# A decoder layer's convolution: 12 odd heads from stored halves in three rounded passes, the others over two shared buffer sets

## What is computed

```python
# k = v = ctx, q = layernorm(x); B = 8, H = 32 heads of 8 channels, L = 512
kv = einsum('bhil,bhjl->bijhl', k_, v_)          # products of channels i, j of a head
y = irfft(rfft(kv, 2 * L) * rfft(ssm_kernel, 2 * L))[..., :L]   # causal convolution over l
out = y + kv * D
out = einsum('bijhl,bhil->bjhl', out, q_)
```

## Time and profile before

| | us |
|---|---|
| median of three runs | 862.4 |
| the three runs | 861.37, 862.4, 862.54 |
| the profiled execution | 863.55 |
| its span, first to last instruction | 861.8 |

### The profile page before, as it was taken

How to read it: one execution, slowest core, us unless ns; L and a number is a source line. 1 busy time by engine, 2 the same in 40 slices (tenths; PEclk the granted TensorE clock), 3 DMA queues, 4 the chain that set the end, 5 groups by cost and what they waited for, 6 DMA issues and landing times.

```text
span 861.8 us, 14219 instructions
## 1 busy us (share of the span) xinstructions
PE 842.3 (98%) x4346; PEld 704.0 (82%) x4346; DVE 543.4 (63%) x849; ACT 377.3 (44%) x608; POOL 445.9 (52%) x439
## 2 busy tenths in 40 slices
PE   8999999999999999999999999999999999999995
PEld 7888888889877777778888778888888888888884
DVE  6767767775657777888769875544455544555431
ACT  5313322333133533442552255555655555655552
POOL 1233223331068899884622343666666666656644
PEclk9999999999999999999999999999999999999998
DMA  8711101100026543440210397989999888999866
GB/s 283 241 39 21 29 24 37 37 12 13 1 62 196 163 131 110 123 131 17 93 63 7 104 323 171 218 204 215 191 189 214 212 213 195 189 196 223 205 119 86
DMA packets 55109, 114.21 MB, mean 133 GB/s; under 512 B 10721, under 2 KB 14817, under 8 KB 54945
## 3 DMA queue, kind: packets, MB, share of 16 engines
q1 hardware_dynamic: 38048, 73.28, 27.6%
q0 software_dynamic: 17024, 40.48, 25.6%
HBM read 83.07 MB, written 30.67 MB: 132 GB/s over the span
## 4 chain that ended last, share of the span: by engine, by line
PE 90%; DVE 5%; issue 2%; POOL 1%; ACT 1%; POOLq 0%; DVEq 0%; ACTq 0%
PE PS L206 20%; PE PS L208 20%; PE PS L207 20%; PE PS L217 17%; PE PS L1645 4%; PE PS L704 2%; PE PS L695 2%; PE PS L633 1%; PE PS L638 1%; PE PS L1582 1%; PE PS L1572 1%; PE PS L1612 1%; PE PS L1581 1%; PE PS L1564 1%; DVE KV L491 0%
## 5 line engine op out<-in xcount | busy, mean ns | idle before, releaser
L206 PE MATMUL PS<-QY_rounded,wh 128*128 128x512 f32 (+1 forms) x376 | 153.8, 409 | 0.0
L208 PE MATMUL PS<-QY_rounded,wl 128*128 128x512 f32 (+1 forms) x376 | 146.4, 389 | 0.0
L1360 POOL DMA_INDIRECT out_y<-QY,idy x72 | 114.5, 1590 | 44.7 <-ACT QY L1454 33.5
L207 PE MATMUL PS<-QY_rounded,wh 128*128 128x512 f32 (+1 forms) x312 | 120.1, 385 | 0.0
L1916 DVE TENSOR_TENSOR hTl<-hh,hTh 128x512 fp32r<-128x512 f32 (+1 forms) x39 | 27.5, 705 | 107.6 <-ACT hTh L1435 107.6
L1337 POOL DMA_INDIRECT xg<-xs_d,idx x64 | 76.7, 1199 | 28.8 <-POOL idx L1333 13.7
L208 PEld LDWEIGHTS PS<-QY_rounded,wl 128*128 128x128 f32 x376 | 71.1, 189 | 15.1
L217 PE MATMUL PS<-qER,Tz 128*128 128x288 f32 x320 | 81.1, 407 | 0.6 <-DVE QY L1062 0.4
L217 PE MATMUL PS<-prod,Tz 128*128 128x288 f32 x320 | 80.5, 407 | 0.2 <-DVE term L1045 0.2
L206 PEld LDWEIGHTS PS<-QY_rounded,wh 128*128 128x128 f32 x376 | 71.3, 190 | 11.1
L1454 ACT ACTIVATE QY<-PS,WPOS 128x512 f32<-128x512 f32 x76 | 52.4, 690 | 55.1 <-PE PS L208 55.1
(11 more groups left out here) (238 smaller groups left out, 1868.8 us busy)
## 6 DMA issues: line engine op xcount, KB each, us to landing
ws<-in_gu_w SPq DMA_DIRECT2D x38, 512.0 KB, 5.6
ws<-in_dn_w SPq DMA_DIRECT2D x20, 512.0 KB, 6.9
C<-in_ctx SPq DMA_DIRECT2D x32, 256.0 KB, 2.6
Tz<-kpad_d SPq DMA_DIRECT2D x32, 256.0 KB, 3.3
xs_d<-xn SPq DMA_DIRECT2D x16, 256.0 KB, 2.0
out_y<-X SPq DMA_DIRECT2D x16, 256.0 KB, 5.7
X<-in_x SPq DMA_DIRECT2D x1, 3072.0 KB, 16.6
xn<-in_xT SPq DMA_DIRECT2D x6, 512.0 KB, 3.3
```

The costliest lines, as they stand in the source:

```text
L206: pe.matmul(out_, lh, rh, start=first, stop=False)
L207: pe.matmul(out_, lh, rl, start=False, stop=False)
L208: return pe.matmul(out_, ll, rh, start=False, stop=last)
L1360: nc.gpsimd.indirect_dma_start(out=out, out_offset=bass.IndirectOffsetOnAxis(ap=idy[:, t:t + 1], axis=0), in_=yo[:, t], in_offset=None, co ...
```

## The change

1. Heads 7, 9, ..., 29 (`HALVES`, 12 of them) are made in three passes of rounded matmuls (`convolve_halves`), 30 of 288 columns each, from high and low halves of the products and of the padded kernel. They have buffers of their own (`odd_h`, `odd_l`, `TzHi`, `TzLo`, two of each), loaded by `load_halves`: four DMAs a head, two of 256 KB and two of 576 KB.
2. The halves of the products are made in the attention part, two heads in each of the steps 1 to 6, and kept in DRAM (`prod_hl_d`): GpSimd makes the products (three instructions a head), ScalarE copies them rounded into a part of `QY` that is not yet used, GpSimd subtracts that from the products in place, and SyncE stores both and loads the next context. The halves of all padded kernels (`kpad_hl_d`) are made once by GpSimd.
3. The other 20 heads (`WHOLE`) stay plain matmuls. Buffers `Tz`, `C2`, `prod` follow their place in that list and not their parity; PSUM banks still follow the parity.
4. The means read back (`mr`) go to `Tz[0]` instead of the last batch of `QY`. Products 0 to 2 are made after the loop. Several weight semaphores are merged into `w_hi` and `w_lo`. The loops of the convolution are written out. The shared low halves are made in six pieces of 512 columns in place of three of 1024. Warming matmuls read weights in place of `aTl`, with the same shape and count.

The diff, cut to its core:

```diff
+AHEAD = 2
+HALVES = [2 * m + 1 for m in range(3, 3 + AHEAD * (B - DIRECT))]
+WHOLE = [h for h in range(CH) if h not in HALVES]
...
-        mr = QY[:, 0:TPB, B - 1]
+        mr = Tz[0][:].rearrange("p (t n) -> p t n", t=TPB)
...
+        NPROD = B * NPAIR
+        ahead_high = QY[:].rearrange("p c b s -> p c (b s)")[:, :, (B - 2) * S:(B - 2) * S + NPROD]
+        ahead_prod = prod[0][:].rearrange("p c b n -> p c (b n)")
+        AHEAD_MADE, AHEAD_LOW, AHEAD_STEP = (3, 7), (4, 8), 8
...
-        def products(pool, i, k):
-
-            pool.wait_ge(c2_in[k], 16 * (i + 1))
-            pool.wait_ge(conv_ps[k], DC * i)
+        def whole_done(eng, n):
+            h = WHOLE[n]
+            eng.wait_ge(conv_ps[h % 2], DC * (h // 2 + 1))
+
+        def products(pool, n):
+
+            k = n % 2
+            pool.wait_ge(c2_in[k], 16 * (B - DIRECT + n // 2 + 1))
+            if n > 1:
+                whole_done(pool, n - 2)
...
+            def store_half(j, m, half, done):
+                sp.dma_start(prod_hl_d[j, bass.ds(m, 1)].rearrange("o p (c n) -> (o p) c n", c=DC), half).then_inc(done, 16)
...
+            def ahead_batch(b, last=False):
+                n = b * AHEAD - DIRECT * AHEAD
+                made = b * AHEAD_STEP - DIRECT * AHEAD_STEP
+                for j in range(AHEAD):
+                    sp.wait_ge(ahead_hi, n + (j + 1))
+                    store_half(0, n + j, ahead_high, hi_out)
+                    sp.wait_ge(ahead, made + AHEAD_MADE[j])
+                    if last:
+                        load_context(sp, WHOLE[j], j)
+                    else:
+                        ahead_context(n + AHEAD + j, j)
+                    sp.wait_ge(ahead, made + AHEAD_LOW[j])
+                    store_half(1, n + j, ahead_prod, lo_out)
...
+            with sp.Fori(DIRECT, B - 1) as b:
+                turned_batch(b)
+                ahead_batch(b)
...
+            def products_ahead(j, s):
+                pool.wait_ge(c2_in[j], s * 16 + 16)
+                wait_apart(pool, lo_out, s * (16 * AHEAD) + 16 * j)
...
+                for half in range(2):
+                    shifted = bass.AP(tensor=a.tensor, offset=a.offset + 2 * half, ap=[a.ap[0], a.ap[1], [1, 2], [1, CD]])
+                    nc.gpsimd.tensor_tensor(o[:, :, 2 * half * CD:2 * (half + 1) * CD].rearrange("p a (s j) -> p a s j", s=2),
+                                            a[:, :, 0:CD].unsqueeze(2).broadcast_to([P, LB, 2, CD]), shifted,
+                                            ALU.mult).then_inc(ahead, 1)
+                nc.gpsimd.tensor_tensor(o[:, :, 4 * CD:], a[:, :, 0:4], a[:, :, 4:8], ALU.mult).then_inc(ahead, 1)
+
+            def low_ahead(j, s):
+                wait_apart(pool, ahead_hi, s * AHEAD + j + 1)
+                nc.gpsimd.tensor_tensor(ahead_prod.bitcast(F32R), ahead_prod, ahead_high, ALU.subtract).then_inc(ahead, 1)
...
             with pool.Fori(DIRECT - 1, B - 1) as b:
                 rstd(pool, 0, b + 1, mv[0][:, :, 1])
+                s = b - (DIRECT - 1)
+                products_ahead(0, s)
+                low_ahead(0, s)
                 wait_apart(pool, xt_mr_in, 32 * b)
...
+                products_ahead(1, s)
                 rstd(pool, 1, b - 1)
+                low_ahead(1, s)
+            wait_apart(pool, lo_out, 16 * len(HALVES))
+            products(pool, 0)
             pool.wait_ge(qp_done, B)
-            products(pool, 0, 1)
+            products(pool, 1)
...
+            def high_ahead(b, j):
+                n = b - (DIRECT - 1)
+                wait_apart(act, ahead, n * AHEAD_STEP + AHEAD_MADE[j])
+                wait_apart(act, hi_out, n * (16 * AHEAD) + 16 * j)
+                act.activation(ahead_high.bitcast(F32R), ahead_prod, ACT.Copy).then_inc(ahead_hi, 1)
...
                 q_evac(b, first)
...
+                if made_ahead:
+                    high_ahead(b, 0)
                 k_evac(b)
...
                         qy_evac(b - 2)
+                    high_ahead(b, 1)
...
+                def load_halves(n):
+                    k = n % 2
+                    for j, (t, dst) in enumerate(((TzHi[k], odd_h[k]), (TzLo[k], odd_l[k]))):
+                        src = bass.AP(tensor=kpad_hl_d.tensor, offset=(j * CH + HALVES[n]) * (KPAD + 1), ap=[[1, P], [1, D]])
+                        sp.dma_start(t[:], src).then_inc(halves_in[k], 16)
+                        sp.dma_start(dst[:].rearrange("p c b n -> p (c b n)"), prod_hl_d[j, n]).then_inc(halves_in[k], 16)
+
+                def next_heads(i):
+
+                    for h in (2 * i, 2 * i + 1):
+                        sp.wait_ge(conv_ps[h % 2], DC * (i + 1))
+                        if h in HALVES:
+                            n = HALVES.index(h) + 2
+                            if n < len(HALVES):
+                                load_halves(n)
+                        else:
+                            n = WHOLE.index(h) + 2
+                            if n < len(WHOLE):
+                                load_toeplitz(sp, WHOLE[n], n % 2)
+                            if 0 < h and n + 1 < len(WHOLE):
+                                sp.wait_ge(prod_done[(n - 1) % 2], 2 * ((n - 1) // 2 + 1))
+                                load_context(sp, WHOLE[n + 1], (n + 1) % 2)
...
+                next_heads(0)
+                load_halves(0)
                 next_heads(1)
+                load_halves(1)
                 sp.dma_start(gw[:], gateT.rearrange("(c p) n -> p c n", p=P)).then_inc(gw_in, 16)
...
+                def convolve_halves(h, behind=None):
+                    n, m = HALVES.index(h), h // 2
+                    k = n % 2
+                    pe.wait_ge(halves_in[k], 64 * (n // 2 + 1))
+                    pe.wait_ge(y_read[1], 2 * m)
+                    for c in range(DC):
+                        o = PS[:, DC + c].rearrange("p (b n) -> p b n", n=YGAP)[:, :, 0:NPAIR]
+                        for r in range(c + 1):
+                            w = slice((c - r) * P, (c - r + 1) * P)
+                            mm = three_pass(pe, o, TzHi[k][:, w].bitcast(F32R), TzLo[k][:, w].bitcast(F32R), odd_h[k][:, r].bitcast(F32R), odd_l[k][:, r].bitcast(F32R), r == 0, r == c)
```

More of the change, by code:

```diff
@@ L328, in _ @@
             pool.wait_ge(xns[1], TPB * B)
-            products(pool, 1, 0)
+            products(pool, 2)
         @block_.scalar
@@ L380, in qy_evac @@
                                    ACT.Copy).then_inc(qy_done, 1)
+            def high_ahead(b, j):
[3 more added lines that the diff above has]
+                act.activation(ahead_high.bitcast(F32R), ahead_prod, ACT.Copy).then_inc(ahead_hi, 1)
             def step(b, first=False, last=False):
+                made_ahead = not (isinstance(b, int) and b < DIRECT - 1) and not last
                 q_evac(b, first)
@@ L753, in _ @@
             transpose_tiles(xn[1], 0, trs[1])
-            convolve(pe, 0, 0, (2, 3))
+            convolve(pe, 0, (2, 3))
             oproj(B - 1, bank=4)
             pe.wait_ge(qy_done, TPB * (B - 1))
-            convolve(pe, 0, 0, (0, 1))
+            convolve(pe, 0, (0, 1))
             for t in range(TPB):
                 pe.wait_ge(x1_done, TPB * (B - 1) + t + 1)
-                warm((5, 3)[t], bank=4 + t)
+                for _ in range((5, 3)[t]):
+                    pe.matmul(PS[:, 4 + t], WH[:, 3, 0, 0:P], WH[:, 3, 0], start=True, stop=True)
                 pe.wait_ge(xns[1], TPB * (B - 1) + t + 1)
@@ L895, in decoder_program @@
         term = [sb2(f"term{k}", [P, CD // 2, LB, CD, 2]) for k in range(2)]
+        odd_h, odd_l = ([sb2(f"odd_{n}{k}", [P, DC, B, NPAIR]) for k in range(2)] for n in ("high", "low"))
+        TzHi, TzLo = ([sb2(f"Tz_{n}{k}", [P, D]) for k in range(2)] for n in ("high", "low"))
         q2_done, term_behind, reduced = sem("q2_done"), sem("term_behind"), sem("reduced")
@@ L928, in _ @@
                     sp.dma_start(out[rows], zrow[:, 0:D]).then_inc(zero_out, 16)
-                with sp.Fori(3 + SLOT_T, normal_head(0) // 2) as i:
+                for i in range(3 + SLOT_T, normal_head(0) // 2):
                     next_heads(i)
@@ L961, in shared_lo @@
                                             ).then_inc(fixed_lo, 1)
-                with pool.Fori(2, 6) as i:
+                for i in range(2, 6):
                     pair_of_heads(i)
@@ L966, in _ @@
                 nc.gpsimd.tensor_tensor(gw_hl[:, :, 1], gw[:], gw_hl[:, :, 0].bitcast(F32), ALU.subtract).then_inc(fixed_lo, 1)
[L967 to L969 removed]
+                for i in range(6, stream_head(0) // 2):
+                    pair_of_heads(i)
+                    shared_lo(i - 6, i - 5)
                 for i in range(stream_head(0) // 2, CH // 2):
[L971 removed]
                     for e in range(EARLY):
@@ L1109, in _ @@
                             pe.wait_ge(xT_lo, e + 1)
-                    convolve(pe, h // 2, h % 2, behind=behind)
+                    if h in HALVES:
+                        convolve_halves(h, behind=behind)
```

(2 more changed lines are left out.)

156 lines of the change are left out of this document (85 added, 71 removed).

## The result

| | before | after |
|---|---|---|
| median of the runs compared | 862.37 us (4 runs, 861.37 to 862.54) | 872.82 us (4 runs, 871.76 to 873.94) |
| ratio | 1 | 1.0118, 95% interval 1.0102 to 1.0134 |
| profiled execution: time, span | 863.55, 861.8 | 873.23, 870.2 |
| start of the eighth batch's v x kp | 224.89 | 235.39 |
| start of the router's matmuls | 399.78 | 408.35 |

The kernel is 10.4 us slower, where 5.2 us less was forecast, and outside the range. The last three rows split it. The attention takes 10.5 us more, the convolution 1.9 less, the rest nothing. Forecast were 2.5 more for the attention and 7.7 less for the convolution (-10.2, +1.3 and +1.2), so that the first was missed by 8.0 us and the second by 5.8.

A forecast was written before the change was run, and what follows sets the result against it. The prediction took TensorE, busy 98% of the span, as the bound, with VectorE and GpSimd near in heads 18 to 28. Its terms, -10.2 + 1.3 + 1.2 + 2.5 = -5.2 us, gave 857.2 us, range 852.0 to 864.5.

The forecast's parts named there:

- 2.5 more for the attention: Attention batches: GpSimd's subtract delays VectorE's X + bias, 0.5 us a batch after slacks in 5 batches; +2.5 us (0 to 10).
- 7.7 less for the convolution: Convolution stage: net of the matmul saving, the VectorE limit and the load wait; 7.7 us less.
- -10.2: Convolution, 12 odd heads in three rounded passes: 4.00 us a head in place of 4.85; -10.2 us (-15.0 to -6.0).
- +1.3: Convolution heads 18 to 27: VectorE needs more time a pair than TensorE will; +1.3 us (0 to 2.7).
- +1.2: Convolution head 6: its Toeplitz block lands late behind head 9's halves and shared weights; +1.2 us (0 to 3).

The follow-up runs named there:

- e8: Changed kernel with head 9's halves loaded after next_heads(2) and one halved head a batch (7 to 17 only) instead of two: 865.50 us, ratio 1.0043.
- e9: e8 with GpSimd's single subtract moved to wait until VectorE has written z's low half: 857.45 us, ratio 0.9949.
- e4: Changed kernel with GpSimd's second subtract of a batch cut to 36 of 1152 columns: 871.08 us, ratio 1.0112.
- e7: Changed kernel, second subtract waiting for the second norm, head 9's halves loaded later, second head's products waiting for z's low half: 858.84 us, ratio 0.9963.
- e5: Changed kernel with GpSimd's products and subtracts for the halves cut to slivers, copies, stores, loads and waits kept: 882.51 us, ratio 1.0238.
- e6: Changed kernel with the loop's stores of halves moving 8 columns in place of 1152, all computing kept: 892.06 us, ratio 1.0329.
- e1: Changed kernel with GpSimd's second subtract of a batch waiting until VectorE has made the second norm: 869.22 us, ratio 1.0081.

## What to carry to other kernels

When work is put on GpSimd beside a chain, list every VectorE instruction that can stand beside each GpSimd instruction, tensor_scalar included, and give the longest GpSimd instructions a place by a wait, behind the instruction that they would block and before ones that read PSUM or take statistics; e8 and e9 differ by nothing else and by 8 us. Then cost what remains by the smallest slack on the chain, not by the idle time of the engine. A wait of TensorE for a load of some 3 us should be costed with the slow matmuls that follow it, and a load that isn't urgent goes behind the first one that is.

## What the runs showed of the hardware

- A tensor_scalar with a single tensor input in SBUF is held by a GpSimd subtract too, and not only one with two: 3.35 against 1.00 us for a pair (L537), and 3.24 against 0.75 in e4 (L564). Statistics over SBUF (0.68) and instructions that read PSUM (at 1.42 in e7; aTl at 1.29 in the changed kernel) kept their times beside the subtracts.
- In these rows the one that starts first keeps its time. In e8 X + bias, starting 0.3 us behind the subtract, takes 4.89 beside it and z; in e7 the one at 130.93, with the subtract following at 131.89, takes 1.29, and the subtract 2.88 instead of 2.68. In the changed kernel GpSimd's small instruction at 130.05 takes 1.19 instead of 0.22 beside a VectorE instruction of 129.94. The rows of e7:

```profile
130.93 1.29 DVE L613 TENSOR_TENSOR X<-X,ob 128x512 f32 x2
...
131.89 2.88 POOL L375 TENSOR_TENSOR prod<-prod,QY 128x1152 fp32r<-128x1152 f32 x1 [1.62 <-ACT QY L464]
```

- After 3.7 us without matmuls TensorE ran near its lower clock level for about one head (0.56 in 286 to 289), which added half of the wait again. Head 6 waited in other runs too: 2.8 us in e5, 3.6 in e4, 4.3 in e6 and 4.5 in e1 were followed by 20 matmuls in 6.78, 6.78, 7.80 and 6.63 us. The idle time of 0.54 before head 4 (changed kernel) had no such effect (5.09 us for 20 matmuls).
